# The order in which two halves of a four-layer attention kernel take turns on each engine: tables worked out anew

## The reference

```python
x = _L0_conv_ref(x, ...)   # latent of 32 channels: softmax(theta'phi) g, then attention to 128 concepts, two 1x1 convs
x = _L1_conv_ref(x, ...)   # q, k of 32 channels, v of 256: softmax(q k) v * gamma + x
x = _L2_conv_ref(x, ...)   # group norm, q, k, v of 256 channels, softmax(q k / 16) v, projection, + x
x = _L3_conv_ref(x, ...)   # group norm, 8 heads of 32 channels, softmax, projection, layer norm, + x
```

## Time and profile before

| | |
|---|---|
| time, median of 3 runs | 2812.36 us (2811.44 to 2816.11) |
| the profiled execution: span | 2818.8 us |
| PE busy | 2605.2 us, 92% |
| DVE busy | 1864.0 us, 66% |
| ACT busy | 1291.2 us, 46% |
| POOL busy | 597.3 us, 21% |
| mean granted TensorE clock | 0.928 of full speed |

### The profile page before, as it was taken

How to read it: one execution, slowest core, us unless ns; L and a number is a source line. 1 busy time by engine, 2 the same in 40 slices (tenths; PEclk the granted TensorE clock), 3 DMA queues, 4 the chain that set the end, 5 groups by cost and what they waited for, 6 DMA issues and landing times.

```text
span 2818.8 us, 26455 instructions
## 1 busy us (share of the span) xinstructions
PE 2605.2 (92%) x9892; PEld 1429.7 (51%) x9892; DVE 1864.0 (66%) x1925; ACT 1291.2 (46%) x2209; POOL 597.3 (21%) x322
## 2 busy tenths in 40 slices
PE   7979988989999999999999999998999999978887
PEld 4556653464644646454564645546464455643332
DVE  4544227687477765777666875868656876568985
ACT  3353221646345462555526454364624546135466
POOL 0083120050110501023020401105010040224473
PEclk8999996989999899999999899998999899989898
DMA  2000010010202002020110202010020200222200
GB/s 88 1 0 1 1 30 16 9 37 1 75 1 45 1 8 68 1 45 1 49 27 1 45 1 75 1 30 16 1 75 1 45 1 16 45 45 46 46 1 30
DMA packets 29297, 72.15 MB, mean 26 GB/s; under 512 B 10224, under 2 KB 10416, under 8 KB 28912
## 3 DMA queue, kind: packets, MB, share of 16 engines
q1 hardware_dynamic: 29168, 70.45, 10.0%
HBM read 11.40 MB, written 8.39 MB: 7 GB/s over the span
## 4 chain that ended last, share of the span: by engine, by line
PE 70%; DVE 17%; ACT 4%; SPq 4%; issue 3%; POOL 2%; DMA 1%; DVEq 0%; ACTq 0%; POOLq 0%
PE ps L632 11%; PE ps L665 11%; PE ps L651 9%; PE ps L783 8%; PE ps L952 7%; PE ps L874 6%; PE ps L640 4%; PE ps L787 4%; DVE ba_nmx L1328 4%; SPq L496 3%; DVE fa_nmx L1328 2%; PE ps L721 2%; PE ps L860 2%; DVE accb L1496 2%; DVE xm L1381 1%
## 5 line engine op out<-in xcount | busy, mean ns | idle before, releaser
L1181 ACT ACTIVATE prb<-ps 128x512 f32<-128x512 f32 x896 | 493.5, 603 | 318.2 <-PE ps L665 294.6
L1328 DVE TENSOR_REDUCE ba_nmx<-ps 128x1 f32<-128x1024 f32 x448 | 529.0, 1218 | 129.4 <-PE ps L651 129.3
L1496 DVE TENSOR_TENSOR accb<-accb,prb 128x1024 f32<-128x1024 f32 x312 | 385.4, 1263 | 90.2 <-ACT prb L1181 89.0
L665 PE MATMUL ps<-qs,ks 97*128 97x512 f32 x896 | 366.1, 484 | 37.2 <-DMA qs<-ba_nmx_r 28.1
L1042 ACT ACTIVATE pr<-ps 128x512 f32<-128x512 f32 x336 | 195.9, 596 | 360.0 <-PE ps L874 271.9
L651 PE MATMUL ps<-ks,qs 96*128 96x512 f32 x896 | 330.2, 475 | 26.5 <-DVE ba_nmx L1328 15.9
L554 POOL TENSOR_TENSOR q2k<-pr,q2k 128x512 fp32r<-128x512 f32 x112 | 145.8, 1318 | 845.6 <-ACT q2k L1079 845.6
L665 PEld LDWEIGHTS ps<-qs,ks 97*128 97x128 f32 x896 | 165.9, 203 | 286.0 <-ACT prb L1181 179.5
L952 PE MATMUL ps<-prb,vb 128*32 128x512 f32 x1792 | 249.5, 630 | 2.6 <-ACT prb L1181 2.5
L651 PEld LDWEIGHTS ps<-ks,qs 96*128 96x128 f32 x896 | 174.9, 210 | 145.9 <-DVE ba_nmx L1328 75.0
L1328 DVE TENSOR_REDUCE fa_nmx<-ps 128x1 f32<-128x1024 f32 x168 | 198.1, 1216 | 47.6 <-PE ps L860 37.1
(11 more groups left out here) (320 smaller groups left out, 3562.3 us busy)
## 6 DMA issues: line engine op xcount, KB each, us to landing
qs<-part SPq DMA_DIRECT2D x168, 128.0 KB, 2.4
ks<-part SPq DMA_DIRECT2D x168, 128.0 KB, 2.4
xm<-in_x SPq DMA_DIRECT2D x8, 1024.0 KB, 5.7
out<-prb SPq DMA_DIRECT2D x28, 256.0 KB, 2.7
q2k<-part SPq DMA_DIRECT2D x48, 128.0 KB, 2.4
w<-in_weights SPq DMA_DIRECT2D x1, 2592.0 KB, 8.8
out<-pr SPq DMA_DIRECT2D x4, 256.0 KB, 2.0
qs<-ba_nmx_r SPq DMA_DIRECT2D x56, 4.0 KB, 1.8
```

The costliest lines, as they stand in the source:

```text
L665: return pe.matmul(o.ps[:, bank, :], keys[0:ROW + 1, tile(jt)], queries[0:ROW + 1, cols(ic)], start=True, stop=True)
L1181: act.activation(weights3(o, s, g), o.ps[:, turn3[score_use(s, g) % 3], :], ACT.Exp)\
L1328: dve.tensor_reduce(o.nmx[:, head, it:it + 1], o.ps[:, bank:bank + 2, :], AX.XY, ALU.max, negate=True).then_inc(o.max_sb[n].sem, 1)
L1496: dve.tensor_tensor(o.sums[pair], o.pairs[(s - 1) % 2][pair] if j == 1 else o.sums[pair], o.pairs[s % 2][pair], ALU.add).then_inc(done.sem, 1)
```

## The change

Twelve of the fifteen tables have other counts; those of SyncE are as before. Each side's slots, their order, instructions and waits stay; only how the two sides are mixed on PE, ACT, DVE and POOL differs. The core of the diff (the tables of *both* for PE, ACT and DVE; those of *fronts* and *backs* change in the same way):

```diff
     ("both", "PE"): (
-        1, 2, 2, 1, 1, 5, 3, 1, 1, 1, 2, 1, 5, 1, 4, 1, 1, 1, 1, 3, 1, 2, 1, 1, 1, 4, 2, 5, 1, 1, 3, 3, 1, 5, 9,
...
-        1, 1, 2, 2, 2, 1, 1, 1, 2, 1, 1, 1, 2, 1, 2, 1,),
+        1, 2, 2, 3, 1, 2, 4, 1, 1, 1, 1, 1, 1, 1, 3, 1, 3, 2, 2, 1, 1, 3, 1, 1, 1, 3, 1, 1, 1, 1, 1, 3, 1, 1,
...
+        1,),
     ("both", "ACT"): (
-        4, 2, 1, 16,),
+        1, 3, 1, 1, 10, 1, 2, 2, 1, 1, 1, 3, 2, 3, 1, 1, 3, 5, 2, 1, 2, 2, 11, 1, 4, 1, 26, 1, 1, 1, 1, 2, 2,
...
     ("both", "POOL"): (
-        0, 26, 1, 6,),
+        1, 32,),
     ("backs", "POOL"): (
-        0, 14, 15, 10, 2, 2, 1, 2, 11,),
+        0, 14, 15, 9, 1, 1, 1, 1, 2, 1, 3, 2, 7,),
```

More of the change, by code:

```diff
@@ L77 @@
     ("fronts", "PE"): (
[19 rows of a table removed]
[20 rows of a table added]
     ("fronts", "ACT"): (
[3 rows of a table removed]
[3 rows of a table added]
     ("both", "ACT"): (
-        1, 2, 1, 1, 1, 1, 10, 1, 2, 2, 2, 2, 1, 2, 1, 3, 1, 2, 1, 1, 1, 2, 1, 3, 2, 1, 13, 1, 5, 1, 25, 3, 1, 1,
-        2, 1, 3, 39, 5, 2, 1, 1, 7, 1, 2, 1, 11, 1, 1, 1, 1, 1, 8, 1, 6, 1, 1, 1, 5, 1, 28, 1, 5, 1, 1, 2, 3, 1,
-        4, 2, 1, 16,),
+        1, 3, 1, 1, 10, 1, 2, 2, 1, 1, 1, 3, 2, 3, 1, 1, 3, 5, 2, 1, 2, 2, 11, 1, 4, 1, 26, 1, 1, 1, 1, 2, 2,
+        1, 3, 39, 6, 3, 4, 1, 6, 1, 6, 1, 1, 1, 7, 1, 2, 1, 5, 1, 6, 1, 5, 1, 27, 1, 1, 1, 4, 3, 5, 1, 3, 1, 2,
+        16,),
     ("backs", "ACT"): (
-        8, 74, 74, 47, 2, 1, 1, 1, 1, 2, 1, 1, 1, 1, 2, 1, 1, 1, 1, 1, 2, 3, 3, 1, 3, 2, 4, 5, 3, 1, 5, 2, 2, 1,
-        4, 1, 4, 1, 1, 1, 1, 2, 3, 1, 6, 2, 8, 1, 6, 1, 12, 1, 5,),
+        7, 2, 1, 69, 4, 2, 4, 1, 66, 47, 2, 2, 4, 2, 3, 1, 1, 1, 4, 2, 2, 2, 6, 2, 4, 2, 2, 2, 6, 2, 3, 1, 2,
+        1, 8, 1, 1, 2, 3, 1, 4, 2, 2, 1, 2, 1, 1, 1, 5, 1, 2, 3, 13, 2, 2,),
     ("fronts", "DVE"): (
-        1, 2, 3, 1, 2, 1, 1, 1, 5, 7, 5, 3, 3, 2, 7, 3, 2, 4, 5, 2, 1, 1, 1, 9, 25, 1, 3, 1, 9, 1, 1, 24, 2, 5,
-        1, 2, 1, 4, 3, 3, 1, 1, 2, 4, 50,),
+        3, 1, 1, 1, 1, 1, 2, 1, 1, 1, 3, 1, 1, 6, 5, 3, 3, 2, 5, 1, 1, 1, 1, 1, 2, 4, 5, 2, 2, 10, 23, 2, 9, 1,
+        2, 1, 4, 35, 1, 1, 1, 1, 2, 1, 6, 3, 1, 1, 49,),
     ("both", "DVE"): (
-        1, 2, 1, 1, 1, 4, 1, 5, 7, 2, 1, 1, 3, 2, 6, 2, 2, 1, 1, 1, 1, 2, 1, 1, 3, 1, 1, 1, 1, 1, 2, 9, 23, 2,
-        2, 1, 2, 1, 8, 17, 7, 1, 2, 3, 4, 2, 1, 1, 2, 1, 3, 1, 1, 2, 4, 2, 6, 3, 1, 1, 42, 1, 5, 1, 1, 1, 5, 1,
-        5, 4, 1,),
[3 rows of a table added]
     ("backs", "DVE"): (
[3 rows of a table removed]
[3 rows of a table added]
     ("fronts", "POOL"): (
-        14, 2, 3, 1, 1, 1, 1, 1, 1, 1, 2, 1, 2, 17, 8, 6, 1, 2,),
+        12, 1, 2, 1, 2, 1, 1, 2, 1, 1, 1, 1, 5, 17, 3, 1, 2, 3, 3, 1, 1, 3,),
     ("both", "POOL"): (
-        0, 26, 1, 6,),
+        1, 32,),
     ("backs", "POOL"): (
-        0, 14, 15, 10, 2, 2, 1, 2, 11,),
+        0, 14, 15, 9, 1, 1, 1, 1, 2, 1, 3, 2, 7,),
     ("fronts", "SP"): (
```

## The result

The changed kernel takes 2772.4 us (median of 4 runs, 2770.51 to 2778.35) against 2814.08 us (4 runs, 2811.44 to 2816.11): a ratio of 0.9855, with a 95% interval of 0.9841 to 0.9869, 41.7 us less. The forecast was 2779, with a range of 2752 to 2806. The profiled execution is the slowest of the four (2778.35 us), as the one of the kernel before was slower than its runs; both traces lie some 6 us over their medians.

What follows compares the result with a forecast made beforehand. PE was taken as the bound, busy 2605.2 of 2818.8 us. Gains of 27 us in the six passes, 1 in the first stage and 5 in the last made 2812.4 - 33 = 2779 us, range 2752 to 2806.

Steps and rivals of the forecast that it cites:

- rival 2: Six passes: less time at 1.2 GHz behind layer 0's maxima, PE gains 5 us more a pass, 2749 us; chance 0.07.
- The bound, and where time can be won: Whole kernel: PE bounds; only its idle 213 us and lower clock can be won, a pass's gains counting six times.
- The turn to layer 2: Each pass: waits before `shift`, `sc0` and `sc2` go; net gain 3.25 us a pass, bounds 1.5 and 4.0.
- The slack of 4.0 us: Turn to layer 2, projection to `sc3`: 3.42 us of waits plus 0.2 us a wait for draining matmuls, in 24.0 us.
- the price at `max7`: Turn to layer 2: in the new order `max7` waits some 0.25 us for maximum 5.
- The 0.5 us given back in the head: Following back's head: fewer front slots between 32 maxima, so maxima wait for DVE, 0.5 us a pass.
- the slots `sc7`, `w5`, `sc8` fill the rest: Back's head, each pass: these front slots cover PE's time until the 24 DMAs allow the first maximum.
- The maxima of layer 0: Each pass: other slots among the maxima, round 0's scores one reduction sooner; gain 1.0 us, bounds -0.5 and 2.0.
- The turn to round 1's scores: Each pass: `u1max31` ahead of `w15`, maxima reach the stack sooner; gain 0.3 us, bounds 0 and 1.4.
- The end of the pass: Each pass: head's last maximum stands last behind `sum1`, wait of 1.05 us stays; gain 0, bounds -0.3 and 0.
- The first and the last stage: Outside the six passes: first stage gains 1 us (bounds -4 and 5), last stage 5 (bounds -3 and 10).
- five maxima of 1.2 us in a stage that DVE paces are 6 us: Last stage, round 0: nine maxima instead of four left for the DMA wait; 6 us, 5 taken for the stage.

Runs made afterwards that it cites:

- turn and head alone: Kernel before, with the new order of the turn to layer 2 and the following back's head in the six passes: ratio 0.9914, 2788.85 us.
- doubled maxima of layer 0: Kernel before, with each of layer 0's eight maxima issuing its two matmuls twice: ratio 0.9965, 2805.95 us.
- the middle alone: Kernel before, with the new order only from the front's slot `s2` to layer 2's first maximum in the six passes: ratio 0.997, 2806.29 us.

## Why the prediction was right, point by point

*The number and its make-up.* The forecast was met within 7 us, and that is in part luck. It took the gain of the passes for waits, 4.55 us each. They gave 6.6, and only 2.3 of these are idle time; the other 4.3 are matmuls that took less time, nearly all by the clock. That is what rival 2, "the clock follows", had, with a chance of 0.07: about half of the forecast's waits and most of rival 2's gain came together, and the sum fell near the forecast.

*The bound, and where time can be won.* Right: the passes gave 40 of the 42 us of span, the first stage 1.3, the last 0.8.

*The turn to layer 2.* Right in mechanism and nearly in size. 3.25 us a pass were forecast (bounds 1.5 to 4.0); turn and head alone give 4.0, 24 us in all, of which 2.7 are idle time; taken out of the changed kernel they cost 17.5, 2.9 a pass, of which 2.3 are idle time. The slack of 4.0 us was measured at 3.9, the price at `max7` 0.25 and 0.22. The 0.5 us given back in the head did not come up. That "the slots `sc7`, `w5`, `sc8` fill the rest" carried more than one sentence showed: without them the turn's gain turns into a loss of 16 us.

*The maxima of layer 0.* This is the step that failed in its mechanism. It had 1.0 us a pass, because round 0's scores can start one reduction sooner. They do start 1.6 us sooner after the opening of the pass, but the waits around them grew from 1.5 to 2.3 us, and PE is idle for 1.4 us a pass more with this order than without. The gain came from the clock, by rival 2. Undone in the changed kernel, layer 0's order costs 13 us (give or take 6), 2.2 a pass; filling PE with useless matmuls at the old order gives 1.6 a pass after their own cost. The second is shown to be the clock's; that the first is the same thing is what the windows say (0.88 and 0.81 to 1.00), and the sizes agree.

*The price of the clock.* Rival 2 took half of the time at 1.2 GHz, 5 us for 10. The runs come near to it where PE is what the others wait for: 0.42 us a microsecond between the changed kernel's second and third pass, 0.4 in the doubled maxima of layer 0, 0.4 behind layer 1's maxima. In the kernel before, passes with 37.5 us at 1.2 GHz take 334.1 us and two with 34.1 take 331.4; of the latter 3.4 us are those at `sc2` that cost nothing, so 6.8 us that count make 2.7, again 0.4 (the remaining pass, with 34.1 and none at `sc2`, takes 333.2). Over the whole span 31.4 us less of busy time go with 69 us less at 1.2 GHz, 0.46 each. Where PE waits for another engine anyway the price is nothing: at `sc2`. "TensorE: Matmul & The Clock Gate" of the Trainium skill, section "HAM oscillation — how this bites in real kernels", has the loss as the time at the lower clock times (1 - 1.2/2.4), which is 0.5; the trace is somewhat under it, and at `sc2` far under it.

*The turn to round 1's scores.* 0.3 us a pass forecast (bounds 0 and 1.4), 1.4 measured for the middle alone. They are waits and not the clock: 0.47 us at the DMA of the maxima (4.68 to 4.21, where the forecast expected 3.3), and most of the rest before round 1's maxima, where two waits for DVE of 0.61 and 0.84 us shrink to 0.14 and two of 0.38 and 0.16. `q0` behind `sum1` stayed at 12.7 us, as the chain said. Which of the moved slots does it was not tried.

*The end of the pass.* 1.07 to 1.32 us: at the bound of -0.3 that the text gave.

*The first and the last stage.* 1 us forecast and 1.3 seen; 5 forecast and 0.8 seen, with a ratio of 1.0003 by itself. The step "five maxima of 1.2 us in a stage that DVE paces are 6 us" failed. They are off DVE, but DVE, at 95% busy before, was not alone in pacing the 59 us; that PE, behind a 10 us wait and at a lower clock, was next is the likely reading and was not tried. At the start the forecast had no gain, and the trace has 2.6 us won and 1.9 given back, the latter by ACT's order and not by the DMAs alone. Image 7's DMAs weigh on both turns of the stage, at 0.63 us per issue as the trace had it (15.20 us for 24), yet the cover bought nothing.

*The sum.* 27 us for the passes were 40; 5 for the last stage were 1; the total of 33 was 42 by the spans and 41.7 by the runs. The errors went opposite ways. A pass's 6.6 us are 2.3 of idle time and 4.3 of busy time, both measured. That the 4.3 are the clock's is an estimate that comes out: 11 us fewer at 1.2 GHz at 0.4 us each.

*The parts don't add up.* Alone: turn and head 24, middle 9, layer 0 1.5, last stage 0, in sum 34 of 41.7. Layer 0 is worth 1.5 us with the old middle, turn and head, and 13 with the new ones.

## What to carry to other kernels

Price an order at its turns, and at each turn list what covers the next DMA or reduction: here 24 DMAs in one queue and their landing take 17 us whoever waits for them, and a turn made shorter is only worth what the slots behind it can cover. A stretch at the lower clock cost here about 0.4 us a microsecond where PE is what the others wait for, and nothing under another engine's wait; two passes of one trace that differ in their clock give the price without a new run. Giving PE useless work in its idle pieces tests where the clock comes from, but what it wins or loses holds the cost of that work too. A row of maxima that looks like idle time on PE may be what keeps DVE fed, so look at DVE's busy time in the same window before spreading it.

## What the runs showed of the hardware that was not expected

More work made the kernel faster: doubling 16 matmuls a pass in PE's idle pieces kept the clock at 2.4 GHz (0.88 and 0.81 to 1.00) and took 9 to 10 us off 2815.3. The same trick at two other places raised the clock (0.80 to 0.90, 0.69 to 0.79) and made the kernel 15 and some 6 us slower, the second at the edge of the noise. Time at 1.2 GHz cost about 0.4 us a microsecond where PE is the bound, and nothing at `sc2`, which starts 5.2 us after `sc0` whether PE is at 1.2 GHz for 3.4 us between them or waits 1.70 us for ACT.
